# Layer 1's experts, the position-bias table and the combination of rows in a fused four-layer model

## The chip, the cores and the metric

The kernel runs on one core of a Trainium2 chip. The metric is the time in device microseconds (us) of one execution.

## The reference

Four layers work on x of shape (2, 1024, 256), 2048 tokens in 16 tiles of 128. Each layer adds a chain of two blocks to x. Layer 1 is a mixture with shared expert followed by a mixture of eight experts; layer 2 is an attention block with a learned relative bias, followed by a product-key block:

```python
# layer 1, second block: 8 experts, 2 per token, width 512
logits = x @ router_w.T;  topk_logits, topk_idx = top_k(logits, 2);  probs = softmax(topk_logits)
hmid = gelu(einsum('th,efh->etf', x, w1) + b1);  y = einsum('etf,ehf->eth', hmid, w2) + b2
out = einsum('eth,te->th', y, combine)            # combine: probs at the chosen experts
# layer 2, first block: bias of 16 heads from the distance of two positions
pos = arange(-n + 1, n)[:, None]
h = silu(ln(pos @ w0 + b0, g0));  h = silu(ln(h @ w1 + b1, g1));  h = h @ w2 + b2
xn = ln(x, g_norm);  q, k, v = projections of xn;  q = l2norm(q) * q_scale;  k = l2norm(k) * k_scale
sim = q @ k.T * 8 + bias, causal;  out = softmax(sim) @ v;  ln(out @ Wout, g_out)
```

## The kernel before

The kernel is a sequence of phases. Each phase gives every engine its own list of instructions, written by hand; engines wait for each other on semaphores; a barrier over all engines ends a phase. Within a phase the work runs tile by tile through `pipeline(eng, n, unroll, *stages)`: at step t an engine does each of its stages for tile t minus the stage's lag, in the order in which the stages are listed. An engine takes its instructions strictly in that order.

The phases that the change touches, in their order, are these.

**Routing of layer 1's experts** (`route_phase`). GpSimd first gathers the rows that the block before wrote (`Gather.rows`, two indirect transfers per tile, 32 in all), VectorE adds them (`Gather.add`, line 976), TensorE transposes the sum and multiplies it by the router's weights, and VectorE chooses two experts per token for groups of four tiles and computes the slots (`choose`, `slots`; line 1344 writes them). GpSimd then scatters each tile's rows into DRAM at its slots, two indirect transfers per tile (line 1122). SyncE loads all eight experts' weights (8 MB, `Experts.load`) and both biases, each as a row repeated over the 128 partitions.

**Layer 1's expert phase** (`kept_experts_phase`, 39 tiles of 128 slots, each with one expert). SyncE loads the tile's rows and stores its results. TensorE transposes the rows (line 1801), multiplies them as the stationary operand by 512 columns of the expert's first weights (line 1810), transposes the activated result (line 1818), and multiplies it by the second weights (line 1827). VectorE adds the first bias (line 1865), ScalarE does the Gelu (line 1846) and copies both transposes out of PSUM (lines 1841, 1851), VectorE adds the second bias (line 1873). TensorE's order is

```python
            pipeline(pe, n_tiles, 4, (0, transpose_x), (2, transpose_h), (1, hidden), (3, outputs))
```

TensorE and VectorE read the number of the tile's expert into a register for each of these operations from tile 8 on.

**The combination phase** (`combine_phase` with `BiasTable`). GpSimd gathers the experts' output rows again (32 transfers), VectorE adds them to x (32 operations). In the same phase the bias table of layer 2 is made: a perceptron of two layers over 1024 positions in 8 tiles, with VectorE (line 2011, then normalising, lines 1993 to 2004), ScalarE (Silu), TensorE (transposes, line 2050; product, line 2056; last product, line 2062) in turn. The additions of rows stand between the table's steps. SyncE then writes the table to DRAM and spreads it with one transfer, in which each of 16 heads gets 128 rows of 1024 numbers, each row starting one number earlier (line 1972). The attention core reads it from there.

**The null phase of layer 2** (`null_phase`): four small loads on SyncE's queue and some ten short operations. Layer 0 has one too, with three loads.

**The projections of layer 2** (`qkv_phase`): SyncE loads the weights, ScalarE and VectorE fold the gain into them, and then for each tile VectorE normalises the rows, TensorE transposes and multiplies them (line 274, 12 passes), ScalarE and VectorE copy the result out (lines 316, 387), ScalarE squares it, VectorE makes the inverse norms and the keys, GpSimd scales the queries (line 451), and TensorE transposes queries and keys (line 287). The product has one set of three PSUM banks.

The attention core (`core_phase`) comes next. Two other phases are used for comparison. `mlp_experts_phase` is layer 0's expert phase: its weights are the stationary operand, ScalarE adds the bias and activates in one operation per 128 columns (line 1559), and the width is 1024, in two PSUM banks, each with its own signal. `glu_experts_phase` has GpSimd copy each tile's weights (768 columns) out of the resident ones (line 1643).

## Time and profile before

| | |
|---|---|
| time, median of 3 runs (range) | 3152.14 us (3149.24 to 3155.32) |
| time of the profiled execution | 3152.37 us |
| span of its trace | 3150.7 us |
| TensorE matmul busy | 2529.1 us (80%) |
| TensorE weight loads busy | 2025.1 us (64%) |
| VectorE, ScalarE, GpSimd busy | 1592.4, 1336.2, 858.2 us (51%, 42%, 27%) |
| DMA, mean over the span | 95 GB/s |

Engines are named PE (TensorE), PEld (its weight loads), DVE (VectorE), ACT (ScalarE), POOL (GpSimd) and SPq (SyncE's queue) in the profile. Shares over the whole span mix phases that have different limits. Instants in the timeline count from the span's start. In brackets at a row's end stands how long the engine was idle before the row, and what ended the wait. PEclk is the granted clock of TensorE as a share of its full speed. The notation `x16` counts the instructions merged into a row.

### The profile page before, as it was taken

How to read it: one execution, taken by the hardware profiler on the slowest of the kernel's cores; microseconds unless marked ns; L12 is line 12 of the kernel's file. 1: busy time of each engine (PE TensorE's matmuls, PEld its weight loads, DVE VectorE, ACT ScalarE, POOL GpSimd, SP SyncE). 2: the span in 40 equal slices, each digit the busy share in tenths (PEclk: the TensorE clock that was granted, in tenths of full speed). 3: DMA queues.
4: the chain of work that ended last, by engine and by line, in shares of the span. 5: the costliest groups of instructions: out<-in, count | busy, mean ns of one | idle time of the engine just before them, and what ended most of it. 6: DMA issues, size and time to landing. Idle time of an engine off the chain costs nothing. (4 is left out here: it accounts for less than half of the span.)

```text
span 3150.7 us, 56089 instructions
## 1 busy us (share of the span) xinstructions
PE 2529.1 (80%) x16160; PEld 2025.1 (64%) x16161; DVE 1592.4 (51%) x4387; ACT 1336.2 (42%) x3092; POOL 858.2 (27%) x1094
## 2 busy tenths in 40 slices
PE   4799999987877827951669999998689998883695
PEld 2477777766777724641347777776667877782685
DVE  3366666545115251233766666654388886435111
ACT  2366666742221502320336566674344443152221
POOL 0132333312014470031133233331243331345002
PEclk9999999997988958976889999999899999795898
DMA  7022132202663461124002212130200000235585
GB/s 259 30 75 77 61 91 68 83 15 116 248 197 83 140 240 50 56 77 141 6 30 68 81 63 89 62 89 16 77 1 1 0 1 11 94 126 187 196 309 178
DMA packets 146656, 298.72 MB, mean 95 GB/s; under 512 B 20822, under 2 KB 106070, under 8 KB 140224
## 3 DMA queue, kind: packets, MB, share of 16 engines
q1 hardware_dynamic: 134208, 265.00, 24.9%
q0 software_dynamic: 12288, 31.83, 3.3%
q8 instruction: 71, 1.16, 0.2%
q14 instruction: 89, 0.73, 0.1%
HBM read 242.33 MB, written 64.56 MB: 97 GB/s over the span
## 5 line engine op out<-in xcount | busy, mean ns | idle before, releaser
L755 DVE CUSTOM_DVE_ANT_0 prob_l<-ps_l,bias_l,nsn 128x1024 f32<-128x1024 f32 (+3 forms) x256 | 276.8, 1081 | 113.1 <-DVEq L754 66.3
L755 DVE CUSTOM_DVE_ANT_0 cur_sb<-ps_h,bias_s,nsn 128x128 f32<-128x128 f32 (+3 forms) x256 | 139.9, 546 | 241.7 <-DVEq L754 241.2
L830 ACT ACTIVATE prob_l<-prob_l,nmax 128x1024 f32<-128x1024 f32 (+3 forms) x256 | 252.0, 984 | 2.4 <-DVE nmax L755 2.1
L686 PE MATMUL ps_l<-khi,stage 128*128 128x512 f32 (+3 forms) x512 | 240.9, 471 | 0.0
L692 PE MATMUL ps_pt<-ident_sb,prob_l 128*128 128x128 f32 x1664 | 231.8, 276 | 5.3 <-DVE pT_l L763 2.8
L814 ACT ACTIVATE cur_sb<-ps_pt 128x128 f32<-128x128 f32 (+3 forms) x256 | 111.1, 434 | 267.4 <-PE ps_pt L692 267.3
L650 POOL COPY nsn<-nsn 128x4 f32 (+1 forms) x128 | 23.9, 187 | 713.1 <-DVE diff L772 570.6
L659 POOL TENSOR_TENSOR stage<-qo,stage 64x256 fp32r<-64x256 f32 x256 | 201.2, 786 | 46.9 <-POOLq L658 46.9
L692 PEld LDWEIGHTS ps_pt<-ident_sb,prob_l 128*128 128x128 f32 x1664 | 186.7, 141 | 29.4 <-ACT cur_sb L814 13.9
L715 PE MATMUL ps_o<-pT_l,v 128*64 128x256 f32 x1664 | 191.6, 380 | 8.7 <-DVE pT_l L763 8.7
L967 POOL DMA_INDIRECT yg<-slot_outputs,slot x128 | 132.3, 1034 | 239.3 <-PEq L88 200.5
L814 ACT ACTIVATE pT_l<-ps_pt 128x512 f32<-128x512 f32 x256 | 153.1, 598 | 78.6 <-PE ps_pt L692 76.0
L274 PE MATMUL ps_q<-wf,xnT 128*128 128x512 f32 (+1 forms) x384 | 144.0, 527 | 49.8 <-ACT xnT L310 49.8
L1559 ACT ACTIVATE hT<-ps_h,mlp_ws 128x128 f32<-128x128 f32 x312 | 89.1, 369 | 223.3 <-PE ps_h L1532 223.2
L686 PE MATMUL ps_l<-klo,stage 128*128 128x512 f32 (+3 forms) x512 | 181.0, 354 | 0.0
L2176 POOL TENSOR_TENSOR ss<-simx,sim 128x4096 f32<-128x4096 f32 x16 | 113.3, 7084 | 242.2 <-DVE simx L2324 242.2
L680 PE MATMUL ps_l<-km,ident 128*128 128x384 bf16 (+5 forms) x512 | 164.5, 321 | 10.2 <-POOL stage L659 10.2
L715 PEld LDWEIGHTS ps_o<-pT_l,v 128*64 128x64 f32 x1664 | 127.0, 137 | 65.7 <-issue 18.4
L1532 PEld LDWEIGHTS ps_h<-xT,mlp_ws 128*128 128x128 f32 x1248 | 148.8, 196 | 2.8 <-DVE xT L1574 0.9
L274 PEld LDWEIGHTS ps_q<-wf,xnT 128*128 128x128 f32 x384 | 69.6, 199 | 125.1 <-issue 111.6
L1532 PE MATMUL ps_h<-xT,mlp_ws 128*128 128x128 f32 x1248 | 149.3, 279 | 0.1
L830 ACT ACTIVATE cur_sb<-cur_sb,nmax 128x128 f32<-128x128 f32 (+3 forms) x256 | 142.6, 557 | 0.0
(334 smaller groups left out, 6075.4 us busy)
## 6 DMA issues: line engine op xcount, KB each, us to landing
mlp_ws<-in_L_ffn_experts_dram SPq DMA_DIRECT2D x39, 2052.0 KB, 7.5
xs<-slot_rows SPq DMA_DIRECT2D x156, 128.0 KB, 2.1
slot_outputs<-ys SPq DMA_DIRECT2D x156, 128.0 KB, 1.9
slot_rows<-zero_sb SPq DMA_DIRECT2D x1, 16384.0 KB, 51.6
bias_l<-in_fside_16xSxS_dram SPq DMA_DIRECT2D x16, 512.0 KB, 3.5
mlp_w<-in_L_ffn_experts_dram SPq DMA_DIRECT2D x8, 1024.0 KB, 15.0
bias_by_partition<-bias_table SPq DMA_DIRECT2D x1, 8192.0 KB, 36.3
bias_l<-bias_by_partition SPq DMA_DIRECT2D x16, 512.0 KB, 3.3
```

What stands on the lines that cost most here:

```text
L274: ins = pe.matmul(ps_q[:, lo:hi], xnT[:, u % 2, k, :], wf[:, k, lo:hi], start=(k == 0), stop=(k == KD - 1))
L659: gp.tensor_tensor(stage[other, x.b, s, hp], q_t, stage[own, x.b, s, hp].bitcast(F32), ALU.subtract).then_inc(gp_s[s].sem, 1)
L680: pe.matmul(out[:, 0:hi - lo - diagonal], c["ident16"][:], att["km"][:, b, lo:hi - diagonal], start=True, stop=False, skip_group_check=True)
L686: ins = pe.matmul(out, stage[:, b, s, x.h % 2, x.h // 2, :], att[part][:, b * S + lo:b * S + hi], start=False, stop=part == "klo", skip_gr ...
L692: ins = pe.transpose(ps_pt[:, bank, (k - first) * P:(k - first + 1) * P], prob[x.s][:, x.h, k * P:(k + 1) * P], c["ident"][:])
L715: ins = pe.matmul(ps_o[hp * DH:(hp + 1) * DH, s * 2 * P:(s + 1) * 2 * P], att["v"][:, x.b * TB + k, :], pT[s][:, k, hp * 2 * P:(hp + 1) * ...
L755: dve.tensor_tensor_reduce(out=spans(x, prob), in0=scored(x), in1=spans(x, bias), scale=-1.0, scalar=nsn[:, b, s, h:h + 1], op0=ALU.add, o ...
L814: act.activation(pT[x.s][:, 0:n, place(x.h)], ps_pt[:, 0, 0:n * P].rearrange("p (k n) -> p k n", n=P), ACT.Copy).then_inc(act_t[x.s].sem, 1)
L830: act.activation(prob[x.s][:, x.h, 0:x.W], prob[x.s][:, x.h, 0:x.W], ACT.Exp, bias=nmax[:, x.b, x.s, x.h:x.h + 1], scale=-1.0, accum_out=r ...
L967: gp.indirect_dma_start(out=yg[:, k, t, :], out_offset=None, in_=self.ys_dram[0:self.n_slots, :], in_offset=bass.IndirectOffsetOnAxis(ap=s ...
L1532: ins = pe.matmul(o, ws[:, u, k * F + f * P:k * F + (f + 1) * P], xT[:, u % 2, k * P:(k + 1) * P], start=(k == 0), stop=(k == KD - 1))
L2176: gp.tensor_tensor(ss[:, u % 2].rearrange("p h (a b) -> p h a b", b=NK), simx[:].unsqueeze(3).to_broadcast([P, HR, NA, NK]), sim[:, 1].uns ...
```

## The change

Four things are done together.

1. In layer 1's expert phase GpSimd copies the tile's weights and the first bias (one column per 128 hidden units) into a ring of four buffers. The first product takes the weights as the stationary operand and the rows as the moving one, so its result is already transposed; ScalarE adds the bias and does the Gelu in four operations of 128 columns, straight out of PSUM. The transposes of the activated result, the separate bias addition and the second copy go. VectorE copies the transposed rows instead of ScalarE.
2. The bias table is made within the routing phase of layer 1's experts, in steps placed among the routing's own steps on VectorE, ScalarE and TensorE. Router logits share a PSUM tile with the transposes there. Its spread to DRAM is issued by GpSimd as its first instruction of the expert phase.
3. The combination phase between layers 1 and 2 is dropped. Its gathers are issued by GpSimd, and its additions done by VectorE, tile by tile in layer 2's projections, whose lists for these two engines are unrolled. The rows land in two buffers that exist already (`c["cur"]` and `r["acc"]`), and the second serves the attention core as a buffer later.
4. The first bias of all experts is loaded in a layout by partition, in elements of 4 bytes.

```diff
@@ qkv_phase, VectorE and GpSimd
+            def combine(t, u):
+                if gather:
+                    if t == 0:
+                        dve_g.open(dve)
+                    gather.add(dve, t, yg, dve_g)
+
             def moments(t, u):
+                if gather:
+                    dve.wait_ge(dve_g.sem, dve_g.after(f"y{gather.choices - 1}", t))
...
-            stages = [(0, moments), (1, normalised)]
+            stages = [(0, combine), (0, moments), (1, normalised)]
...
-                pipeline(gp, NT, 4, (0, normalised))
+                def fetched(t, u):
+                    gather.rows_of_tile(gp, yg, t)
+
+                if gather:
+                    unrolled(gp, NT, 4, (0, fetched), (4, normalised))
+                else:
+                    pipeline(gp, NT, 4, (0, normalised))
@@ route_phase, TensorE
+            def bias_table(t, u):
+                if table is None:
+                    return
+                if t == 3:
+                    table.turn(pe, 1)
+                if t == 5:
+                    table.second_product(pe)
+                if t == 8:
+                    table.turn(pe, 2)
+                if t == 10:
+                    table.last_product(pe)
+
-            pipeline(pe, NT, NT, (late, turned), (S_AT + 2, down), (L_AT, logits), (S_AT, gate_up), (R_AT, ranks))
+            pipeline(pe, NT, NT, (late, turned), (S_AT + 2, down), (L_AT, logits), (S_AT, gate_up), (R_AT, ranks), (0, bias_table))
@@ route_phase, VectorE
+            def bias_table(t, u):
+                if table is None:
+                    return
+                if t == 1:
+                    table.first_layer(dve)
+                if t == 2:
+                    table.normalise(dve, 1)
+                if t == 4:
+                    table.turned_half(dve, 1)
+                if t == 6:
+                    table.second_layer(dve)
+                if t == 7:
+                    table.normalise(dve, 2)
+                if t == 9:
+                    table.turned_half(dve, 2)
+
             pipeline(dve, NT, NT, (0, combine), (0, norm), (L_AT + 1, logits), (S_AT + 1, hidden), (L_AT + 1, choose),
-                     (R_AT + 1, slots))
+                     (R_AT + 1, slots), (0, bias_table))
@@ kept_experts_phase
+        @block.gpsimd
+        def _(gp):
+            table_dram, spread_dram, spread_done = bias_spread
+            gp.dma_start(spread_dram, bass.AP(table_dram.tensor, table_dram.offset + P - 1,
+                                              [[S + P, H], [-1, P], [1, S]])).then_inc(spread_done, 16)
+            gp_w.open(gp)
+            gp.wait_ge(experts.sem, experts.count)
+
+            def weights(t, u):
+
+                e = experts.of(gp, r, t)
+                gp.wait_ge(pe_y.sem, pe_y.after("y", t - 4))
+                gp.wait_ge(gp_w.sem, gp_w.after("weights", t - 1))
+                gp.sem_inc(gp_w.sem, 1)
+                gp.tensor_copy(b1s[:, u], at(experts.vectors[0], e)).then_inc(gp_w.sem, 1)
+                gp.tensor_copy(ws[:, u], at(experts.w, e)).then_inc(gp_w.sem, 1)
+
+            pipeline(gp, n_tiles, 4, (0, weights))
...
             def hidden(t, u):
-                e = experts.of(pe, r, t)
-                pe.wait_ge(act_x.sem, act_x.after("xT", t))
-
-                pe.wait_ge(dve_h.sem, dve_h.after("pre", t - 2))
-                for k in range(KD):
-                    ins = pe.matmul(ps_h[:, u % 2, 0:F], xT[:, u % 2, k * P:(k + 1) * P],
-                                    at(experts.w, e)[:, k * F:(k + 1) * F], start=(k == 0), stop=(k == KD - 1))
+                pe.wait_ge(dve_x.sem, dve_x.after("xT", t))
+                pe.wait_ge(gp_w.sem, gp_w.after("weights", t))
+                pe.wait_ge(act_h.sem, act_h.after("h", t - 2))
+                for f in range(FC):
+                    for k in range(KD):
+                        ins = pe.matmul(ps_h[:, u % 2, f * P:(f + 1) * P], ws[:, u, k * F + f * P:k * F + (f + 1) * P],
+                                        xT[:, u % 2, k * P:(k + 1) * P], start=(k == 0), stop=(k == KD - 1))
                 ins.then_inc(pe_h.sem, 1)
...
-            pipeline(pe, n_tiles, 4, (0, transpose_x), (2, transpose_h), (1, hidden), (3, outputs))
+            pipeline(pe, n_tiles, 4, (0, transposes), (2, outputs), (1, hidden))
...
             def hidden(t, u):
-                act.wait_ge(dve_h.sem, dve_h.after("pre", t))
-                act.wait_ge(pe_t.sem, pe_t.after("hT", t - 2))
-                act.activation(h[:, u % 2, :], pre[:, u % 2, :], func).then_inc(act_h.sem, 1)
...
+                act.wait_ge(pe_h.sem, pe_h.after("h", t))
+                for f in range(FC):
+                    ins = act.activation(hT[:, u % 2, f * P:(f + 1) * P], ps_h[:, u % 2, f * P:(f + 1) * P], func,
+                                         bias=b1s[:, u, f:f + 1])
+                ins.then_inc(act_h.sem, 1)
```

ScalarE has table steps in the routing too: a root at steps 1 and 6, Silu at 3 and 8, the other half of the turned table at 4 and 9, the last bias at 11. SyncE loads the table's weights ahead of the experts' and stores the table behind them.

## Rows read from the trace of the kernel before

**Rows 1.** Windows view: one stretch of the expert phase, and the combination phase.
```profile
core 0: us, PE busy (x) PEld busy (x) DVE busy (x) ACT busy (x) POOL busy (x), PEclk, DMA share, GB/s
1205.00:1370.00 165.00, 154.27 (x635) 101.83 (x635) 39.09 (x70) 57.22 (x108) 0.00 (x0) 1.00 0.17 54
1386.00:1452.00 66.00, 19.71 (x72) 14.40 (x72) 39.21 (x97) 12.71 (x11) 34.21 (x33) 0.65 0.27 79
```

**Rows 2.** Timeline of layer 1's expert phase: start, length, engine, line, operation.
```profile
1191.76 5.42 SPq L1779 DMA_DIRECT2D xs<-slot_rows  x5
...
1196.46 3.78 PE L1810 MATMUL ps_h<-mlp_w,xT 128*128 128x512 f32 x4
...
1214.64 0.42 DVE L1873 TENSOR_TENSOR ys<-ps_y,mlp_v 128x256 f32<-128x256 f32 x1 [1.04 <-PE ps_y L1827]
...
1369.42 0.42 DVE L1873 TENSOR_TENSOR ys<-ps_y,mlp_v 128x256 f32<-128x256 f32 x1 [1.03 <-PE ps_y L1827]
```

**Rows 3.** Timeline of the combination and null phases.
```profile
1386.26 0.35 SPq L1962 DMA_DIRECT2D w<-in_L_cond_w_dram  x1
...
1452.86 14.90 SPq L474 DMA_DIRECT2D m<-in_mask_BxS_bf_dram  x1
...
1492.82 0.38 SPq L244 DMA_DIRECT2D w<-in_L_cond_Wq_dram  x1
```

**Rows 4.** DMA issues on the page: KB each, us to landing.
```profile
bias_by_partition<-bias_table SPq DMA_DIRECT2D x1, 8192.0 KB, 36.3
```

**Rows 5.** Timeline of the null phase of layer 0.
```profile
10.05 0.35 SPq L474 DMA_DIRECT2D m<-in_mask_BxS_bk_dram  x1
...
18.11 0.38 SPq L244 DMA_DIRECT2D w<-in_L_cond_Wq_dram  x1
```

**Rows 6.** Timeline of the routing of layer 1's experts.
```profile
1131.57 0.18 DVE L1344 CAST slot_out<-rk 128x4 uint32<-128x4 f32 x1
...
1142.97 1.03 POOL L1122 DMA_INDIRECT slot_rows<-cur_sb,slot_out  x1 [0.30 <-issue]
...
1143.44 0.17 DVE L1344 CAST slot_out<-rk 128x4 uint32<-128x4 f32 x1
...
1182.86 0.98 POOL L1122 DMA_INDIRECT slot_rows<-cur_sb,slot_out  x1 [0.30 <-issue]
```

**Rows 7.** Groups by line, VectorE, combination phase: busy us, mean ns.
```profile
L976 DVE SCALAR_TENSOR_TENSOR x_sb<-yg,wt,x_sb 128x256 f32<-128x256 f32 x32 | 14.4, 476 | 0.6
```

**Rows 8.** Timeline of VectorE in the combination phase.
```profile
1406.47 2.29 DVE L2004 TENSOR_TENSOR h<-h,g 128x2048 f32<-128x2048 f32 x1
...
1414.54 1.23 DVE L2016 COPY hT<-ps_bias 128x1024 f32<-128x1024 f32 x1 [3.94 <-PE ps_bias L2050]
...
1424.64 2.29 DVE L2019 TENSOR_TENSOR h<-ps_bias,b 128x2048 f32<-128x2048 f32 x1 [7.05 <-PE ps_bias L2056]
```

**Rows 9.** Groups by line, GpSimd's copies, whole kernel.
```profile
L1643 POOL COPY ws<-glu_w 128x768 f32 x62 | 51.3, 827 | 51.0 <-POOLq L1642 51.0
...
L2169 POOL COPY xs<-cur_sb 128x256 f32 x12 | 15.7, 1311 | 0.0
```

**Rows 10.** Timeline of the MLP expert phase of layer 0.
```profile
842.39 3.62 PE L1543 MATMUL ps_y<-mlp_ws,hT 128*128 128x256 f32 x16
...
845.85 3.73 PE L1532 MATMUL ps_h<-xT,mlp_ws 128*128 128x128 f32 x32
...
849.42 0.38 PE L1522 MATMUL ps_x<-ident_sb,xs 128*128 128x128 f32 x2
...
849.62 1.14 ACT L1559 ACTIVATE hT<-ps_h,mlp_ws 128x128 f32<-128x128 f32 x4 [0.64 <-PE ps_h L1532]
```

**Rows 11.** Timeline of layer 2's projections.
```profile
1597.95 0.91 DVE L387 COPY raw<-ps_q 128x512 f32<-128x512 f32 x2 [0.51 <-PE ps_q L274]
...
1605.29 0.91 DVE L387 COPY raw<-ps_q 128x512 f32<-128x512 f32 x2 [0.41 <-PE ps_q L274]
...
1608.89 5.88 PE L274 MATMUL ps_q<-wf,xnT 128*128 128x512 f32 x12 [1.95 <-ACT xnT L310]
...
1614.32 0.91 DVE L387 COPY raw<-ps_q 128x512 f32<-128x512 f32 x2 [2.19 <-PE ps_q L274]
```

More of the change, by code:

```diff
@@ L216, in qkv_phase @@
         weights, tabled, folded = ph.sem(), ph.sem(), ph.sem()
+        if gather:
+            dve_g = ph.steps(" ".join(f"y{k}" for k in range(gather.choices)))
         dve_0 = ph.steps("stats waited moments")
@@ L532, in core_phase @@
         prob = (ph.sb("prob_l", [P, 4, LONG * P]), spare[0])
-        pT = (ph.sb("pT_l", [P, LONG, 4 * P]), spare[1])
+        pT_l = ph.sb("pT_l", [P, LONG, 4 * P]) if rows is None else rows[:].rearrange("p (k two) d -> p k (two d)", two=2)
+        pT = (pT_l, spare[1])
         oT = ph.sb("oT", [P, 4 * P])
@@ L1095, in _ @@
                     sp.dma_start(dst[:], src_.rearrange("(k p) n -> p k n", p=P)).then_inc(shared_in, 16)
+            if table:
+                table.load(sp)
             if experts is not None:
                 experts.load(sp)
+            if table:
+                table.store(sp)
             if first_weights is not None:
@@ L1717, with __init__ @@
 class Experts:
-    def __init__(self, nc, ctx, name, arrived, w, vectors=()):
+    def __init__(self, nc, ctx, name, arrived, w, columns=None, rows=None):
         E = w.shape[0]
@@ L1762, in kept_experts_phase @@
         stores = [ph.sem() for _ in range(4)]
+        gp_w = ph.steps("expert bias weights")
         pe_x = ph.steps("xT")
-        act_x = ph.steps("xT")
+        dve_x = ph.steps("xT")
         pe_h = ph.steps("h")
-        dve_h = ph.steps("pre")
         act_h = ph.steps("h")
-        pe_t = ph.steps("hT")
-        act_t = ph.steps("hT")
         pe_y = ph.steps("y")
@@ L1874, in outputs, with combine_phase @@
                                   ).then_inc(dve_y.sem, 1)
-            pipeline(dve, n_tiles, 4, (1, hidden), (3, outputs))
-def combine_phase(nc, pool, c, gather, out=None, bias_table=None):
+            pipeline(dve, n_tiles, 4, (0, transposed), (2, outputs))
+def combine_phase(nc, pool, c, gather, out=None):
     G = 4
     with Phase(nc, pool) as ph:
-        yg = ph.sb("yg", [P, gather.choices, NT, D])
+        yg = [ph.sb(f"yg{k}", [P, NT, D]) for k in range(gather.choices)]
         dve_g = ph.steps(" ".join(f"y{k}" for k in range(gather.choices)))
         stored = ph.sem()
-        table = BiasTable(nc, ph, c, *bias_table) if bias_table else None
         block = ph.stack.enter_context(nc.Block())
@@ L2007, in vector, with then, row_moments, first_layer @@
+    def then(self, dve, ins):
+        self.count += 1
+        ins.then_inc(self.v, 1)
+        dve.wait_ge(self.v, self.count)
+    def row_moments(self, dve):
+        for t in range(S // P):
+            ins = dve.bn_stats(self.stats[:, t, :], self.h[:, t, :])
+        self.then(dve, ins)
+        for t in range(S // P):
+            ins = dve.bn_aggr(self.mv[:, t, :], self.stats[:, t, :])
+        ins.then_inc(self.moments, 1)
+    def first_layer(self, dve):
         dve.wait_ge(self.made, 1)
-        then(dve.tensor_copy(self.pos[:], self.pos_i[:]))
+        self.then(dve, dve.tensor_copy(self.pos[:], self.pos_i[:]))
@@ L2020, in vector @@
[L2020 to L2035 removed]
+        for t in range(S // P):
+            ins = dve.scalar_tensor_tensor(self.h[:, t, :], self.rows["w0"][:], self.pos[:, t:t + 1], self.rows["b0"][:],
+                                           ALU.mult, ALU.add)
@@ new lines, in first_layer, with normalise @@
+        self.then(dve, ins)
+        self.row_moments(dve)
+    def normalise(self, dve, n):
+        h = self.h
+        dve.wait_ge(self.rooted, n)
+        self.then(dve, dve.reciprocal(self.rstd[:], self.sd[:]))
+        for t in range(S // P):
+            ins = dve.tensor_scalar(h[:, t, :], h[:, t, :], self.mv[:, t, 0:1], self.rstd[:, t:t + 1], ALU.subtract, ALU.mult)
+        self.then(dve, ins)
+        dve.tensor_tensor(h[:], h[:], self.rows[f"g{n - 1}"][:].unsqueeze(1).to_broadcast([P, S // P, D]),
+                          ALU.mult).then_inc(self.normed, 1)
@@ new lines, in turned_half, with second_layer, root @@
+    def turned_half(self, dve, n):
+        dve.wait_ge(self.turned, n)
+        dve.tensor_copy(self.hT[:, 1, :], self.ps_t[:, 1, :]).then_inc(self.out_t, 1)
+        if n == 2:
+            dve.memset(self.table[:, S:], 0.0).then_inc(self.cleared, 1)
+    def second_layer(self, dve):
+        dve.wait_ge(self.product, 1)
+        self.then(dve, dve.tensor_tensor(self.h[:], self.ps_h, self.rows["b1"][:].unsqueeze(1).to_broadcast([P, S // P, D]), ALU.add))
+        self.row_moments(dve)
+    def root(self, act, n):
+        act.wait_ge(self.moments, n)
+        act.activation(self.sd[:], self.mv[:, :, 1], ACT.Sqrt, bias=self.c["eps"][:, 0:1]).then_inc(self.rooted, 1)
```

299 lines of the change are left out of this document (130 added, 169 removed).

## The prediction

> **What bounds the kernel now.** I read the windows by phase first, then the timeline of each phase that the edit touches, then the groups by line. The kernel is a string of phases with barriers between them, so each has its own bound. In layer 1's expert phase TensorE is busy 154 of 165 us at full clock [rows 1]; finished tiles leave VectorE at 1214.64 and, 33 tiles later, at 1369.42: 4.69 us each [rows 2]. The combination phase is the opposite: TensorE 19.7 of 66 us, no engine above 60% [rows 1]. It is a serial walk through the bias table, from its first load at 1386.26 to the null phase's first load at 1452.86, 66.60 us [rows 3]. The null phase lasts to 1492.82, because its loads stand behind the 8192 KB spread transfer, which takes 36.3 us to land; the load right behind it takes 14.90 us to issue [rows 3, 4]. The same phase in layer 0, with nothing ahead of it, takes 8.06 [rows 5]. The routing phase is bound by GpSimd: 32 gathers, then 32 scatters from 1142.97 to 1182.86, 1.287 us apart, without a pause. So its end is set by when a group's slots are ready against GpSimd's need: group 0's at 1131.75 against 1142.97 (11.2 us to spare), group 1's at 1143.61 against 1142.97 + 10.3 = 1153.3 (9.7) [rows 6].
>
> **Removed.** The combination phase goes: 66.60. The spread moves one phase up, so the null phase's 39.96 becomes layer 0's 8.06 plus 0.5 for a fourth load: 31.4 [rows 3, 5]. Together 98.0.
>
> **The table moved into routing.** VectorE was busy 39.2 us in the combination phase, 14.4 of it the 32 additions [rows 1, 7]: 24.8 us of table work enters its queue in steps 1 to 9, nearly all ahead of group 0's slots (step 8). Behind each of its waits stand the additions, the choice and the slots. I laid the queues out in order. Step 1 can start at 1112; the table's loads go out ahead of the experts' and are there. The first layer takes VectorE to 1119, normalising to 1125.4. At step 4 it waits for Silu and the transposes, 5.8 us in all [rows 8], to 1131.2; at step 6 for the second product, 8.9 us [rows 8] after the halves are copied and TensorE has done its own step 5: 1143.4. The second layer ends at 1149, its normalising at 1155.5, and group 0's slots come at 1158.4, so the scatters start 15.7 us late. Group 1's slots came 11.9 behind group 0's [rows 6]; with the second half to copy and TensorE's last product ahead of the logits they come 15.2 behind, at 1173.6, where GpSimd wants them at 1169.0: 4.7 more. Groups 2 and 3 are in time. Routing: +20.5. Bounds: +14 if group 1 fits too and a little is absorbed, +27 if all of the 26.7 us by which group 0 slips is felt. ScalarE's table switches lie in its idle time. The bias in 4096 pieces of 4 bytes instead of a broadcast is priced by no row; it has 80 us before anything waits for it, so I cost it at nothing; without that cover the start of the expert phase would slip by what is left of it, and I allow 2 us for gathers that it slows.
>
> **The spread on GpSimd's queue.** It is GpSimd's first instruction in the expert phase; the copy of the first tile's weights is queued behind it, and the first product waits for that copy. An indirect transfer of 128 rows costs GpSimd 1.03 us [rows 6], 8.0 ns a row; the spread has 16 x 128 = 2048 rows, 16.4 us. Bounds: the price of one issue, 1 us, and 36, if GpSimd stands until the data has landed [rows 4]. SP's next load took 14.90 us to issue behind these 2048 rows [rows 3], near 16.4, so I take that. GpSimd copies 768 columns in 827 ns [rows 9], hence 2048 in 2.2 at most; with the bias copy and the gaps 2.7. The first product moves from 1196.46 to the phase's start, 1191.4 (its first load is issued at 1191.76) + 16.4 + 2.7 = 1210.5 [rows 2]: +14.0. At 1 us the copy is there before the row tiles: 0. At 36: +33.6.
>
> The Trainium skill (DMA: Bandwidth & Descriptors, section Anatomy of one DMA, SWDGE (gpsimd) path) says that generating descriptors is small and that many can be emitted before the cost shows. By that page the spread costs GpSimd next to nothing and the sum is 14.0 lower; no row here shows a plain transfer issued by GpSimd.
>
> **The expert tile.** TensorE loses the four transposes and the dynamic expert reads; the first product becomes 16 passes of 128 columns. The MLP phase has this form: 32 such passes run from 845.85 to 849.42, so 16 take 1.79; 16 passes of the second product run from 842.39 to 845.85, so 8 take 1.73 [rows 10]; two transposes 0.22. TensorE's work falls to 3.74. But its order is transposes(t), outputs(t-2), hidden(t-1): a tile's outputs follow its own hidden product with one pair of transposes between. ScalarE's four Gelu wait for the whole product (one signal), start 0.20 behind it and take 1.14 [rows 10]; TensorE's next pass runs later by an allowance of 0.16. In the MLP phase a second bank covers this; here nothing does. Period: 1.79 + 0.20 + 1.14 + 0.16 + 1.73 = 5.02 for 4.69, +0.33 on 38 periods, 12.5, less about 2.8 for a drain that is one step shorter: +9.7. GpSimd's 2.7 per tile and VectorE's two operations hide below 5.02; with ScalarE's part covered the tile would take 3.74.
>
> **Projections of layer 2.** VectorE gets two additions per tile, 0.48 each [rows 7] and their waits: 1.04. The loop runs TensorE, VectorE's copy, ScalarE, TensorE: 7.34 us from copy to copy (1597.95 to 1605.29), or 9.03 (to 1614.32) where the clock falls and twelve passes take 5.88, four steps of the twelve in the timeline; in the fast step VectorE waits only 0.41 for its copy [rows 11]. 7.34 - 0.41 + 1.04 is 7.97, some 7.9 with waits that close: VectorE becomes the bound in the eight fast ones. 8 x 0.55 = 4.4, two additions before the first transposes 2.1, the ends 1.5: +8. Bounds: +2, the start alone, and +18, if every step goes the slow way. Gathers take GpSimd 2.6 a tile, in its wait for VectorE, and the first is due before the weights are folded.
>
> **Sum.** -98.0 + 20.5 + 14.0 + 9.7 + 8 = -45.8. The profiled execution took 3152.37 us (span 3150.7), the median is 3152.14: one frame. Forecast 3106.5.
>
> **Rivals.**
> - The spread's issue is cheap on GpSimd: 3092.5. No row prices it; against it stand 8 ns a row. 0.27.
> - GpSimd stands until the spread has landed, +33.6 for +14.0: 3126. SP's queue did stand behind it. 0.10.
> - The clock falls in the expert phase. TensorE idles 1.28 of 5.02 us there; in the projections it idles 1.95 and one step in three costs 1.69 more [rows 11]. 13 such tiles, +22: 3128.5. Against: shorter gaps. 0.13.
> - ScalarE's part is covered and a tile takes 3.74: 38 x 1.28 less, 3058. Against: the one signal. 0.04.
> - The other side: the weight copies bind. That outweighs the gain from 45.8 / 39 + 5.0 = 6.2 us a tile. One row points there: 256 columns in 1.31 us [rows 9], 10.5 for 2048, 11.0 a tile, 39 x 6.0 = +234: 3340. But those copies follow a long addition beside a busy VectorE, and the 768-column ones, in an expert phase like this, took 827 ns on the mean of all. 0.04.
>
> The Trainium skill (SBUF — State Buffer, section Who interferes with whom) holds that VectorE shuts GpSimd out only with two SBUF inputs or in a two-port mode. VectorE's operations in this phase read PSUM, so by that page the last rival falls; no run has shown it.
>
> **Numbers.** Forecast 0.40, rivals as given, 0.02 left. All terms at their low ends give -98 + 14 + 0 + 9.7 + 2 = -72 (3080), all at their high ends +13. Eight in ten lie in 3080 to 3132. A measurement of this kernel tells 0.2%, 6.3 us, from no change: faster 0.94, same 0.02, slower 0.04.
>
> **What would show it.** No combination phase and a null phase of 9 us; first scatter near 1158 and a pause before the ninth; the first hidden product some 19 us behind the expert phase's first load; a period of 5.0 with TensorE waiting 1.3 a tile for ScalarE; fast projection steps at 7.9. I am wrong if routing grows by under 10 us, if the period is far from 5.0, or if GpSimd's first weight copy is immediate or 30 us late.

## The result, and the profile after

The changed kernel takes 3100.57 us (median of 4 runs, 3096.48 to 3102.75), the kernel before 3150.69 beside it (4 runs). The ratio is 0.9841 with a 95% interval of 0.9819 to 0.9863: 50.1 us less, 1.6%. The profiled execution took 3096.48 us, span 3094.8, so the two profiled spans are 55.9 apart. Timelines put 51.4 of that in the stretch that the edits touch (the attention core's first bias load moved from 1642.88 to 1591.44); the other 4.5 lie behind it, in phases that the edits leave alone, and are not counted as theirs.

Timeline of the routing and the start of the expert phase, changed kernel (start, length, engine, line, operation, idle time before it and what ended it):

```profile
1143.58 1.00 POOL L1002 DMA_INDIRECT yg<-slot_outputs,slot  x1 [0.30 <-issue]
...
1158.50 0.17 DVE L1417 CAST slot_out<-rk 128x4 uint32<-128x4 f32 x1
...
1159.63 1.10 POOL L1165 DMA_INDIRECT slot_rows<-cur_sb,slot_out  x1 [15.06 <-DVEq L1418]
...
1174.14 0.17 DVE L1417 CAST slot_out<-rk 128x4 uint32<-128x4 f32 x1
...
1175.16 1.17 POOL L1165 DMA_INDIRECT slot_rows<-cur_sb,slot_out  x1 [4.93 <-DVEq L1418]
...
1205.52 0.98 POOL L1165 DMA_INDIRECT slot_rows<-cur_sb,slot_out  x1 [0.31 <-issue]
...
1214.52 3.93 SPq L1875 DMA_DIRECT2D xs<-slot_rows  x5
1214.82 1.10 POOL L1890 DMA_DIRECT2D bias_by_partition<-bias_table  x1 [8.32 <-POOLq L91]
...
1216.04 1.91 POOL L1902 COPY ws<-mlp_w 128x2048 f32<-128x2048 f32 x1
...
1218.05 3.34 PE L1924 MATMUL ps_h<-xT,ws 128*128 128x128 f32 x16 [0.37 <-DVE xT L1962]
...
1302.56 1.99 PE L1933 MATMUL ps_y<-ws,hT 128*128 128x256 f32 x8 [1.02 <-ACT hT L1947]
1304.39 1.95 PE L1924 MATMUL ps_h<-xT,ws 128*128 128x128 f32 x16
...
1306.37 1.14 ACT L1947 ACTIVATE hT<-ps_h,b1s 128x128 f32<-128x128 f32 x4 [3.87 <-PE ps_h L1924]
...
1307.57 1.99 PE L1933 MATMUL ps_y<-ws,hT 128*128 128x256 f32 x8 [1.01 <-ACT hT L1947]
...
1423.61 0.35 SPq L505 DMA_DIRECT2D m<-in_mask_BxS_bf_dram  x1
...
1432.87 0.38 SPq L257 DMA_DIRECT2D w<-in_L_cond_Wq_dram  x1
```

The reader is to see four things against [rows 2, 3, 6]. GpSimd stands 15.06 us between its last gather and its first scatter, which before followed each other at once, and 4.93 ahead of group 1. The 8192 KB spread costs GpSimd 1.10 us, and the first product starts 3.53 us behind the first row load (4.70 before). A tile takes 1302.56 to 1307.57, 5.01, and TensorE waits 1.0 of it for ScalarE. The combination phase is gone, and the null phase takes 9.26 us.

Windows of the changed kernel: most of the expert phase, and two steps of layer 2's projections.

```profile
core 0: us, PE busy (x) PEld busy (x) DVE busy (x) ACT busy (x) POOL busy (x), PEclk, DMA share, GB/s
1230.00:1400.00 170.00, 133.75 (x868) 118.95 (x869) 28.13 (x67) 38.40 (x135) 66.59 (x66) 1.00 0.24 79
1471.14:1478.75 7.61, 4.81 (x20) 2.67 (x19) 7.22 (x18) 3.38 (x7) 3.94 (x3) 1.00 0.12 36
1478.75:1487.91 9.16, 7.02 (x25) 3.77 (x24) 7.32 (x19) 4.25 (x10) 3.94 (x3) 0.81 0.10 29
```

TensorE is busy for 79% of the expert phase, where it was 93% [rows 1], and the clock stays at 1.00, the 2.4 GHz level. In a fast step of the projections VectorE is now busy 7.22 of 7.61 us; the rest is gaps of up to 0.15 between its own operations.

A table from the timelines, with those of the experiments below. Routing is the first gather to the last scatter, the expert phase its first row load to the next phase's first load, the projections their first load to the core's first bias load. Only the first row has a combination phase, of 66.60 us. A time with (1) is that of one execution.

| kernel | time, us | ratio to before | routing | expert phase | null | projections |
|---|---|---|---|---|---|---|
| before | 3150.69 | 1 | 82.52 | 194.50 | 39.96 | 150.06 |
| changed | 3100.57 | 0.9841 (0.9819 to 0.9863) | 104.73 | 209.09 | 9.26 | 158.57 |
| outputs_last | 3053.14 | 0.969 (0.9673 to 0.9706) | 105.97 | 164.92 | 9.25 | 159.04 |
| old_tile | 3096.72 (1) | | 104.65 | 202.38 | 9.16 | 158.86 |
| spread_on_sync | 3127.04 (1) | | 105.80 | 238.90 | 9.24 | 159.21 |
| table_spaced | 3087.46 | 0.9795 (0.9779 to 0.9811) | 96.45 | 209.97 | 9.58 | 158.31 |
| copied_twice | 3071.08 (1) | | 104.92 | 175.08 | 8.94 | 161.66 |
| spread_by_pairs | 3066.22 | 0.9717 (0.9697 to 0.9738) | 104.50 | 177.72 | 8.97 | 161.87 |
| best | 3051.44 | 0.9673 (0.9656 to 0.9691) | 87.70 | 177.03 | 8.98 | 161.55 |
| adds_on_gpsimd | 3097.38 (1) | | 104.42 | 208.99 | 9.31 | 160.93 |
| eight_row_tiles | 3048.51 | 0.9668 (0.9642 to 0.9693) | 105.41 | 154.58 | 9.25 | 161.63 |
| best_2 | 3025.51 | 0.9604 (0.9588 to 0.9619) | 88.26 | 154.21 | 9.28 | 158.60 |
| all_heads_pieces | 3044.63 (1) | | 107.01 | 154.58 | 9.08 | 161.67 |
| best_3 | 3029.20 | 0.9602 (0.9581 to 0.9623) | 88.43 | 154.70 | 9.10 | 159.47 |

Single times move by several us: executions of the kernel before, taken beside these runs, took 3142.70 to 3163.98. The phase columns are steadier, and most verdicts below rest on them. The projections are an example of why: where their lists are the changed kernel's, they take 158.3 to 161.9, with five to seven of their steps over 8.5 us, where the clock is lower for a part.

### The profile page after: what moved, and what is told of

Read it like the earlier page. It is cut to its first block and busy times, and to the rows that moved or that the text cites. A ratio compares the mean times of both kernels' runs of the same rounds, so it can differ in the third digit from the quotient of the medians.

```text
span 3094.8 us, 56173 instructions
## 1 busy us (share of the span) xinstructions
PE 2512.4 (81%) x16472; PEld 2048.1 (66%) x16472; DVE 1589.5 (51%) x4387; ACT 1318.4 (43%) x3132; POOL 940.5 (30%) x1173
## 5 line engine op out<-in xcount | busy, mean ns | idle before, releaser
L712 PE MATMUL ps_l<-km,ident 128*128 128x384 bf16 (+5 forms) x512 | 164.4, 321 | 10.2 <-POOL stage L691 10.2
L1002 POOL DMA_INDIRECT yg<-slot_outputs,slot x96 | 100.2, 1044 | 228.6 <-PEq L88 200.0
L1632 PE MATMUL ps_y<-mlp_ws,hT 128*128 128x256 f32 x624 | 144.9, 386 | 0.0
L1632 PEld LDWEIGHTS ps_y<-mlp_ws,hT 128*128 128x128 f32 x624 | 117.9, 194 | 15.4 <-issue 0.2
L724 PE MATMUL ps_pt<-ident_sb,cur_sb 128*128 128x128 f32 x640 | 116.8, 280 | 6.2 <-ACT pT_l L846 3.0
## 6 DMA issues: line engine op xcount, KB each, us to landing
slot_rows<-zero_sb SPq DMA_DIRECT2D x1, 16384.0 KB, 51.4
bias_by_partition<-bias_table POOLq DMA_DIRECT2D x1, 8192.0 KB, 36.6
```

The costliest lines, as they stand in the source:

```text
L712: pe.matmul(out[:, 0:hi - lo - diagonal], c["ident16"][:], att["km"][:, b, lo:hi - diagonal], start=True, stop=False, skip_group_check=True)
L724: ins = pe.transpose(ps_pt[:, bank, (k - first) * P:(k - first + 1) * P], prob[x.s][:, x.h, k * P:(k + 1) * P], c["ident"][:])
L1002: gp.indirect_dma_start(out=yg[k][:, t, :], out_offset=None, in_=self.ys_dram[0:self.n_slots, :], in_offset=bass.IndirectOffsetOnAxis(ap=s ...
L1632: ins = pe.matmul(ps_y[:, u % 2, 0:D], hT[:, u % 2, f * P:(f + 1) * P], ws[:, u, w2 + f * D:w2 + (f + 1) * D], start=(f == 0), stop=(f == ...
```

## The experiments

**Outputs last.** TensorE's order within a step, in the expert phase only:

```
-            pipeline(pe, n_tiles, 4, (0, transposes), (2, outputs), (1, hidden))
+            pipeline(pe, n_tiles, 4, (0, transposes), (1, hidden), (2, outputs))
```

> Only the order of TensorE's steps in layer 1's expert phase changes: transposes(t), hidden(t-1), outputs(t-2), so that a tile's Gelu has another tile's outputs, transposes and first product beside it. Theory (the 5.04 us period is a ring through ScalarE, 1.2 us of it TensorE's wait): the period falls to TensorE's own work in the changed kernel's timeline, 1.83 from outputs to first product, 1.78 to the transposes and 0.2, so 3.8 us; 38 periods save about 46 us, 3100.6 to 3054. Rival A (the ring only moves: GpSimd's copy of 2.1 us plus its wait for a buffer, or SyncE's row loads, bind next): the period stops between 4.2 and 4.8, 3065 to 3090. Rival B (the 5.04 was not ScalarE's part): the period stays within 0.1 of 5.04 and the time within 0.2% of 3100.6.

Measured: the phase 164.92 for 209.09 us, the kernel 3053.14. The theory's number to the microsecond. Windows and timeline of this kernel:

```profile
1245.00:1370.00 125.00, 125.00 (x867) 116.40 (x866) 25.56 (x66) 38.17 (x134) 64.58 (x64) 0.99 0.22 72
```

```profile
1228.65 0.36 SPq L1875 DMA_DIRECT2D xs<-slot_rows  x1
...
1241.81 0.69 PE L1915 MATMUL ps_x<-ident_sb,xs 128*128 128x128 f32 x2 [7.63 <-DMA xs<-slot_rows]
...
1249.82 1.89 PE L1933 MATMUL ps_y<-ws,hT 128*128 128x256 f32 x8
...
1253.55 1.89 PE L1933 MATMUL ps_y<-ws,hT 128*128 128x256 f32 x8
```

TensorE is busy in all of 125 us, and a tile takes 3.73. So the order alone took 1.3 us off each tile, and the wait for ScalarE's four Gelu is gone; neither the weight copies nor the row loads hold the steady tile (rival A). The timeline also shows what came next: once the tiles are fast, one row load, issued at 1228.65, is not there when TensorE wants it, and finished tiles are 13.7 us apart at that place instead of 3.7. That is 10.0 us, which the expectation did not have. Its number came out right because the period fell further than it said (from 5.04 to 3.73, not 3.8) and the drain is shorter (the last two gaps are 3.52 and 1.72 us, where the changed kernel keeps 5.07).

**The old tile form.** The expert phase of the kernel before in the changed kernel, with the spread on GpSimd:

```
-                kept = Experts(..., columns=a["L1_ffn_b1"], rows=a["L1_ffn_b2"])
+                kept = Experts(..., (a["L1_ffn_b1"], a["L1_ffn_b2"]))
 @@ kept_experts_phase: as before, and
+        @block.gpsimd
+        def _(gp):
+            gp.dma_start(spread_dram, bass.AP(...)).then_inc(spread_done, 16)
```

> Layer 1's expert phase is the one of the kernel before (rows stationary, four transposes of the result, no copies of weights, first bias loaded by broadcast), with the spread still issued by GpSimd as the phase's first instruction; all else as changed. Theory (the new tile form costs the phase 14.6 us as traced, 209.1 against 194.5 from first load to next phase's first load): the phase takes 194.5 again, the period is 4.69, and the kernel comes to about 3086. Rival (what grew is the phase's surroundings, the spread's transfer beside the row loads among them): the phase stays above 200 us. If the bias load in 4-byte elements matters at all, the routing phase shortens here by more than 1 us.

Measured: the phase takes 202.38, between the two kernels: 7.9 us over the phase before and 6.7 under the changed one. The rival was right, and it says where 7.9 us come from:

```profile
1235.46 0.36 SPq L1868 DMA_DIRECT2D xs<-slot_rows  x1
...
1238.49 0.42 DVE L1968 TENSOR_TENSOR ys<-ps_y,mlp_v 128x256 f32<-128x256 f32 x1 [1.03 <-PE ps_y L1922]
...
1245.77 0.69 PE L1896 MATMUL ps_x<-ident_sb,xs 128*128 128x128 f32 x2 [7.52 <-DMA xs<-slot_rows]
...
1252.82 0.42 DVE L1968 TENSOR_TENSOR ys<-ps_y,mlp_v 128x256 f32<-128x256 f32 x1 [1.07 <-PE ps_y L1922]
```

A row load issued while the spread is under way takes over 10 us (12.5 in the changed kernel, below; the 27 us that the expectations further on give it are wrong), and finished tiles are 14.33 us apart instead of 4.7. That is 9.6 us, of which a faster start gives 1.8 back: the first finished tile comes 16.1 us behind the first row load for 17.95. So the spread is not free with this tile form; in the changed kernel, whose tiles take 5.0 for another reason, it costs only 1.2 (one gap of 6.25), and the other 13.4 of its 14.6 us belong to the tile form. The routing takes 104.65 here and 104.73 in the changed kernel: loading the bias in 4-byte elements costs nothing that the profile shows.

**The spread on SyncE.** The same transfer, moved ahead of the row loads in the other list:

```
 @block.gpsimd
-            gp.dma_start(spread_dram, bass.AP(...)).then_inc(spread_done, 16)
 @block.sync
+            sp.dma_start(spread_dram, bass.AP(...)).then_inc(spread_done, 16)
```

> The spread is issued by SyncE ahead of the row loads, not by GpSimd; nothing else changes. Theory (the 14.90 us that a load took to issue behind the 2048-row transfer belongs to SyncE's hardware queue, and GpSimd's software queue has no such stand): the row loads come 15 us late, the first product moves from 3.5 to about 19 us behind the phase's first instruction, and the kernel takes about 3115. Rival (the stand came from the barrier or from loads that read the same rows, not from the queue): the row loads go out at once and the time stays within 0.2% of 3100.6.

```profile
1210.85 0.69 SPq L1882 DMA_DIRECT2D bias_by_partition<-bias_table  x1
...
1211.85 35.09 SPq L1875 DMA_DIRECT2D xs<-slot_rows  x5
...
1245.02 1.12 PE L1915 MATMUL ps_x<-ident_sb,xs 128*128 128x128 f32 x4 [58.82 <-DMA xs<-slot_rows]
```

DMA view of the spread and of the first row load behind it, us to landing:

```profile
bias_by_partition<-bias_table SPq DMA_DIRECT2D x1, 8192.0 KB, 33.8
xs<-slot_rows SPq DMA_DIRECT2D x1, 128.0 KB, 33.1
```

The first product comes at 1246.3, 35 us behind the phase's first instruction, and the kernel takes 3127. The theory had the place right and the size wrong. On the same queue the first row load does not only stand for its issue (12.66 us here, 14.90 in [rows 3]); it is issued 1.0 us behind the spread, lands 33.1 us later, and so comes 0.3 us after the spread's end. Issued by GpSimd, the spread leaves the first five row loads alone.

**The table's steps spaced.** Steps of the bias table within the routing, with the same work:

```
 VectorE:  first layer 1, normalise 2 -> 3, half 4 -> 7, second layer 6 -> 14,
           normalise 7 -> 17, half 9 -> (ScalarE copies both halves)
 TensorE:  turn 3 -> 5, second product 5 -> 11, turn 8 -> 19, last product 10 -> 20
 ScalarE:  root 1 -> 2, Silu 3 -> 4, half 4 -> 6, root 6 -> 15, Silu 8 -> 18, halves 9 -> 19, last bias 11 -> 20
```

> The bias table's steps within the routing are set further apart and behind the slots of groups 0 and 1: VectorE first layer at step 1, normalising at 3, turned half at 7, second layer at 14, second normalising at 17 (the second pair of halves is copied by ScalarE alone); TensorE's second product at step 11, its last two at 19 and 20. The same work is done. Theory (routing grew by 22 us because group 0's slots stand behind waits and work that need not be ahead of them; 9 us of GpSimd's slack was unused): group 0's slots come near 1140, the first scatter at once behind the last gather (no wait of 15 us), and one pause of about 6 us is left ahead of group 2; the last scatter comes about 8 us later than in the kernel before, in place of 22.7, and the kernel takes about 3086. Rival (VectorE's 24.8 us of work bind wherever it stands): the last scatter comes over 18 us late and the time is within 0.2% of 3100.6. Rival (the chain's length binds: the table ends after the last scatter): the scatters end early but the expert phase starts no more than 6 us earlier than in the changed kernel.

```profile
1147.77 1.00 POOL L1002 DMA_INDIRECT yg<-slot_outputs,slot  x1 [0.30 <-issue]
1149.07 1.02 POOL L1165 DMA_INDIRECT slot_rows<-cur_sb,slot_out  x1 [0.30 <-issue]
...
1153.63 9.49 PE L2140 MATMUL ps_bias<-w,hT 128*128 128x256 f32 x32
...
1179.27 0.98 POOL L1165 DMA_INDIRECT slot_rows<-cur_sb,slot_out  x1 [9.82 <-DVEq L1428]
```

The first scatter follows the last gather at once, as the theory has it, but the pause ahead of group 2 is 9.82 and not 6: group 2's logits stand behind 9.49 us of second product in TensorE's list, and VectorE waits. Routing 96.45, 8.3 under the changed kernel and not 14. The time, 3087.46 for 3086 expected, fits better than its reason: the median is 13.1 under the changed kernel, of which the routing shows 8.3 (the profiled execution took 3093.70). Neither rival holds: the work fits, its order cost.

**Weights copied twice**, on top of outputs last:

```
+                gp.tensor_copy(again[:], at(experts.w, e)).then_inc(gp_w.sem, 1)
                 gp.tensor_copy(ws[:, u], at(experts.w, e)).then_inc(gp_w.sem, 1)
```

> Outputs last, with GpSimd copying each tile's weights once more, into a buffer that nobody reads. Theory (the copy costs 1.89 us and hides until GpSimd's tile is longer than TensorE's 3.74): GpSimd needs 0.15 + 0.13 + 2 x 1.9 = 4.1 us a tile, the period becomes 4.1 to 4.2, and the phase grows by 33 x 0.4 = 14 us over outputs last, to about 3068. Rival (copies disturb VectorE's or TensorE's access to the buffers): the period is well over 4.3. Rival (GpSimd's price per copy grows when it never rests): copies over 2.1 us.

The phase grows by 10.2 us to 175.08 (14 expected, and 3068 for the 3071.08 of this one execution): 1.8 ahead of the first product, which now waits for two copies, and 8.1 in the tiles. From the sixteenth on, when the ring's lead is used up, tiles take 3.93 to 4.25. Windows:

```profile
1300.00:1370.00 70.00, 68.41 (x445) 59.74 (x443) 13.32 (x35) 19.39 (x68) 65.86 (x52) 1.00 0.20 64
```

GpSimd is busy 65.86 of 70 us, and each copy still takes 1.89. The theory holds and neither rival does. The copies bind only when GpSimd's tile passes TensorE's: here it is 4.09 on the mean for two copies, 0.31 beside them. By these numbers, as an estimate, a single copy would have to take 3.4 us, and not 1.89, before it costs anything at 3.73 a tile.

**The spread in pieces of two heads**, on top of outputs last: eight DMAs ahead of the copies of tiles 4, 6, ... 18.

```
+                if 0 <= h < H and h % 2 == 0:
+                    gp.dma_start(spread_dram[h:h + 2], bass.AP(table_dram.tensor, table_dram.offset + h * (S + P) + P - 1,
+                                                               [[S + P, 2], [-1, P], [1, S]])).then_inc(spread_done, 16)
```

> On top of the reordered TensorE steps (outputs last), GpSimd issues the spread not whole at the start of the expert phase but two heads at a time (1 MB, an eighth of it) ahead of the weight copies of tiles 4, 6, ... 18; GpSimd's list is unrolled for it. Theory (the transfer costs nothing at its issue but holds the next row loads for 27 us behind it: one gap of 13.7 us between finished tiles in place of 3.7, so 10 us): each piece holds the queues about 4.6 us (36.6 / 8), less than the two tiles (7.5 us) between pieces and less than the lead of the row loads, so no gap is over 5 us and the kernel comes to 3053 - 10 = 3043. Rival (row loads are late whenever pieces are under way): eight gaps of 1 to 2 us, and 3049 to 3053.

A miss: 177.72 for the phase, 12.8 us worse than the whole spread. The pieces delay tiles by 0.5 to 2 us each, and the last costs 13.6 us alone. DMA view of the phase (1214 to 1393 us), of the last piece, and of the software queue from 1228 to 1231 us, when only the first piece was under way on it:

```profile
q0 software_dynamic: 16512, 8.45, 16.2%
...
bias_by_partition<-bias_table POOLq DMA_DIRECT2D x8, 1024.0 KB, 12.7
...
bias_by_partition<-bias_table POOLq DMA_DIRECT2D x1, 1024.0 KB, 26.0
...
q0 software_dynamic: 34, 0.14, 12.4%
```

One line of its timeline:

```profile
1302.85 1.05 POOL L1896 DMA_DIRECT2D bias_by_partition<-bias_table  x1 [18.79 <-issue]
```

GpSimd stood 18.79 us before an issue that takes 1.05. And one piece kept 12.4% of the 16 DMA engines' time, two sixteenths. Against the whole spread the size, the place and the shape had all changed; the shape was the next suspect.

The 12.7 us to landing is too kind to this form. All eight pieces count on one semaphore, and at 1235.5, where the profile puts the landing of the first, only 108 packets of 4 KB had gone through the queue, where a piece has 256. The last piece has none behind it: its 26.0 us are the price of one.

**First combination of the gains**: outputs last, pieces of two heads, the table spaced, and the second product in quarters at steps 8, 9, 12 and 13.

> Three edits together: outputs last, the spread in eight pieces, and the table's steps spaced in the routing as before, with TensorE's second product split into quarters at steps 8, 9, 12 and 13 (the wait of VectorE for it was 6 us in the spaced version). Theory: the spaced routing took 8.3 us off the changed kernel's; the split takes the pause ahead of group 2's scatters from 9.5 us to 3 at most, 6 more; with 3043 for the other two the kernel comes to 3043 - 8 - 6 = 3029. Rival (the chain of the table ends too late for the split to help): 3035. Rival (the gains do not add): over 3040.

3051.44, where 3029 was expected: the rival that the gains do not add was nearest, and the phases say why. The routing went to 87.70, so the quarters took 8.8 us more off it; the expert phase took 177.03, 12 us more than with the whole spread, where the pieces were to save 10.

**The additions on GpSimd**, in layer 2's projections of the changed kernel:

```
-            stages = [(0, combine), (0, moments), (1, normalised)]
+            stages = [(0, moments), (1, normalised)]
-                    unrolled(gp, NT, 4, (0, fetched), (4, normalised))
+                    unrolled(gp, NT, 4, (0, fetched), (2, combine), (6, normalised))
```

Each addition becomes a product and an addition there.

> The changed kernel with the combination's two additions per tile in layer 2's projections done by GpSimd (a product with the weight, then an addition, each twice) instead of VectorE; GpSimd gathers, adds two tiles behind, and normalises six behind. Theory (VectorE, busy without a gap for 7.62 us, is the bound of the fast steps): the fast step falls to the 7.34 us of the kernel before or a little under, and the projections shorten by 8 x 0.28 plus the 2.1 us at the start, 154 us in place of 158.6. Rival (GpSimd becomes the bound: 2.6 for two gathers, 1.9 for normalising, four operations of 256 columns at 0.3 to 1.3 each): steps of 8 us or more and projections over 160 us. Rival (the loop is not VectorE's): no change within 1 us.

Steps of 7.43 to 7.47 instead of 7.62, so VectorE was the bound. But a tile then has 1.9 + 2.4 + 3.3 us of work for GpSimd, which takes 7.90 us from tile to tile without a rest; the first copy of results comes 3.8 us later (28.6 us behind the first load for 24.8), and the projections take 160.9. Nothing is gained: the rival that GpSimd becomes the bound is the nearest.

**Eight row tiles**, on top of outputs last: the spread whole, ahead of the fourth weight copy, and twice the ring.

```
-        xs = ph.sb("xs", [P, 4, D])
+        xs = ph.sb("xs", [P, 8, D])
-            pipeline(sp, n_tiles, 4, (0, load), (4, store))
+            pipeline(sp, n_tiles, 8, (0, load), (8, store))
```

> Outputs last, the spread whole again but issued by GpSimd ahead of its fourth weight copy (some 7 us into the phase), and a ring of eight row tiles in place of four: SyncE loads eight tiles ahead, and its stores are issued eight tiles behind in its list. Theory (the only cost of the spread is that row loads issued behind it land 27 us later, and the row ring of four covers 11 to 15 us of that): nine row tiles are in or under way ahead of it, 9 x 3.74 = 34 us of work, so the gap of 13.7 us between finished tiles is gone and the kernel comes to 3053 - 10 = 3043. Rival (stores, held behind the spread too, bind instead because the output ring has four buffers): a gap of 5 to 15 us at VectorE's addition, waiting for a store, and 3048 to 3060.

```profile
1254.13 0.42 DVE L1970 TENSOR_TENSOR ys<-ps_y,mlp_rows 128x256 f32<-128x256 f32 x1 [4.14 <-DMA slot_outputs<-ys]
```

The phase takes 154.58, 10.3 less: the theory. Of the rival's wait for a store a little is seen, as in this line, in two gaps of 4.65 and 5.20, made good behind it. The time, 3048.51, has the widest range of all (3039.88 to 3057.05), and its interval (0.9642 to 0.9693) overlaps that of outputs last (0.9673 to 0.9706), so the time alone does not show the gain. The phase does. In the profiled execution, 3053.24 for 3052.98 with outputs last, what was gained there was lost again where this edit touches nothing: the routing ended 2.7 later, the projections took 2.6 more, and the rest lies behind them.

**The second combination**: this, with the table spaced and the product in quarters.

> The same with the table's steps spaced and the second product in quarters, whose routing took 87.7 us from the first gather to the last scatter in the version before this one, against 104.7 in the changed kernel. Theory: 3043 - 17 = 3026. Rival (stores bind as above): 3031 to 3043.

3025.51, 0.9604 of the kernel before, for 3026 expected.

**Pieces of all heads**: as the pieces of two heads, but 16 partitions of all 16 heads each.

```
-                    gp.dma_start(spread_dram[h:h + 2], ... [[S + P, 2], [-1, P], [1, S]])
+                    q = h // 2 * (P // 8)
+                    gp.dma_start(spread_dram[:, q:q + P // 8, :], ... [[S + P, H], [-1, P // 8], [1, S]])
```

> The spread in eight pieces at the same places as before, but each piece is 16 partitions of all 16 heads (outermost dimension 16) and not all partitions of two heads (outermost dimension 2). Theory (the pieces of two heads were slow because of their shape: 12.7 us to landing for 1 MB, 17.5 thousand packets in the phase's software queue where the whole spread leaves 3.0, and the last one stood 18.8 us on GpSimd for it): a piece lands in 4.6 us (36.6 / 8) or a little more, none stands, no gap between tiles is over 5 us, the phase takes some 155 us in place of 177.7, and the kernel takes 3043. Rival (pieces of 1 MB are slow whatever their shape, since GpSimd makes their descriptors): 12 us to landing and 3060 or more again.

DMA view of the phase (1213 to 1369 us), and of the software queue from 1224.5 to 1227 us, with one piece under way:

```profile
q0 software_dynamic: 2176, 8.39, 15.5%
...
bias_by_partition<-bias_table POOLq DMA_DIRECT2D x8, 1024.0 KB, 5.9
...
q0 software_dynamic: 237, 0.97, 95.3%
```

The same 1 MB, the same places in GpSimd's list, 5.9 us to landing for 26.0, and the phase 154.58 for 177.72. Shape alone, then. The last line says how: one piece now has 95.3% of the 16 engines' time, where one of two heads had 12.4%. The 14336 packets more in the other form are no smaller rows. They bring 0.06 MB, 4 bytes each; the rows go in packets of 4 KB in both.

**The third combination**: the same in place of the ring of eight.

> The version with the spaced table, outputs last, a ring of four row tiles, and the spread in pieces of 16 partitions. Theory: 3026, the same as with the ring of eight row tiles and the whole spread, since both leave TensorE nothing to wait for. Rival as above: 3045 or more.

3029.20, 0.9602, with an interval that holds the second combination's. Its windows show that the expert phase has nothing left but TensorE's own work:

```profile
1225.00:1320.00 95.00, 95.00 (x659) 88.42 (x659) 19.55 (x50) 29.64 (x104) 53.18 (x56) 1.00 0.40 133
```

## Why the prediction was right, and where it was not

The direction and the time were right (3106.5 forecast, 3100.57 measured, range 3080 to 3132), but the sum holds one wrong term and one that is too small, which cancel in part. That the time came within 6 us is in part luck: one term was 15.2 us too large, and the others together 9.1 too small.

- **Removed**: 98.0 forecast, 97.3 measured. 66.60 went whole; the null phase takes 9.26 where I had 8.56.
- **Routing**: +20.5 forecast, +22.2 measured. Group 0's slots were done at 1158.67 (forecast 1158.4) and group 1's at 1174.31 (1173.6); the pause ahead of group 1 is 4.93 (4.7). Some 1.4 us come from scatters that took longer than the 1.287 apart. The mechanism, waits and work queued ahead of the slots, is shown by the spaced table: the same work in another order, with the second product in quarters, took 16.3 to 17.0 us off.
- **The spread on GpSimd's queue**: the step that failed. I took 8.0 ns a row from indirect transfers [rows 6], 16.4 us, and +14.0 for the first product. It took 1.10 us, and the first product came 1.2 us earlier than before, relative to the phase's first load. The rival that the issue is cheap was right on this term, and by the prediction's own sign it was wrong here: the first weight copy starts at 1216.04, right behind the issue. The price of 8.0 ns a row came from an indirect transfer, and a plain one of 2048 rows does not pay it. The Trainium skill (DMA: Bandwidth & Descriptors, section Anatomy of one DMA, SWDGE (gpsimd) path) says that many descriptors can be emitted before their cost shows, which agrees with the 1.10.
- **What the spread costs instead** was in no part of the prediction. The transfer of 8192 KB takes 36.6 us to land and most of the DMA engines' time meanwhile, and a row load among it lands late. In the changed kernel this costs 1.2 us and is covered by the slow tile. DMA view of the changed kernel from 1226 to 1232 us:

```profile
q0 software_dynamic: 457, 1.87, 98.5%
q1 hardware_dynamic: 3, 0.00, 0.1%
issues: line engine op xcount, KB each, median us to landing
slot_outputs<-ys SPq DMA_DIRECT2D x1, 128.0 KB, 10.6
xs<-slot_rows SPq DMA_DIRECT2D x1, 128.0 KB, 12.5
```

The store was issued at 1228.19 and the row load at 1229.47, so this stretch does not show how the two queues share; from 1232 to 1236 us both move packets:

```profile
q0 software_dynamic: 280, 1.15, 86.6%
q1 hardware_dynamic: 201, 0.19, 14.0%
```

- **The expert tile**: +9.7 forecast, +15.8 measured. The period was right, 5.04 for 5.02, and so was its cause. What was mis-sized is the drain, -2.8: the start did become 3.7 us shorter (9.52 from the first product to the first finished tile, 13.25 before), but the kernel before ended fast, its last tiles 4.3 to 1.7 us apart, 5.2 us under the steady pace, and the new order keeps 5.07 to the end. That makes +1.4. The period gives 38 x 0.35 = 13.3, the spread's gap 1.2.
- **Projections**: +8 forecast, +8.5 measured: fast steps at 7.62 (forecast 7.9, 7.34 before), and the first copy of results 3.9 us later, where I had 2.1 and 1.5 for the ends. The other 4.6 are in the steps: the fast ones cost half of what was forecast, and five run slow for four before.

The measured terms: -97.3 + 22.2 + 0.1 + 14.6 + 8.5 = -51.9 (the 14.6 are -1.2 for the first product, 15.8 for the tiles), and the routing began 0.45 later: -51.4, as traced. The clock did not fall in the expert phase (1.00 there, TensorE idle for 1.0 us of 5.0). The weight copies took 1.89 each and bound nothing; the Trainium skill (SBUF — State Buffer, section Who interferes with whom) lets them run free beside VectorE's reads of PSUM, and all 39 copies of the changed kernel lie between 1.890 and 1.907 us.

The gain of 50 us left 75 more in place (3100.57 to 3025.51). The phases show 44 of them in the order of TensorE's steps, 16 in the order of the table's and 10 in the spread; the other 5 lie outside the phases of the table.

## What to carry to other kernels

When a product's result goes through another engine before the next product reads it, put the next tile's product between the two in TensorE's list; look at the wait in one steady tile, since an average of 79% busy does not say that one line's order costs a quarter. A big transfer moved to a cheap place is still paid by the small ones beside it: count how many microseconds of loads are in hand when it starts, and cut it into pieces whose outermost dimension has sixteen entries. Work moved into another phase's lists costs by what is queued behind it, so place each step behind the last thing that has a deadline before it, and cut a long one into parts.

## What the hardware showed that I had not expected

- A plain DMA of 2048 rows of 4 KB costs GpSimd 1.10 us to issue, as much as an indirect one of 128 rows (1.00). But with eight pieces of the bad shape the last issue stood 18.79 us, until 1302.85, when the seventh (issued at 1275.13, 27.3 us to landing) had landed; what it waited for in the queue was not tried.
- The shape of a transfer of the same size set its speed: 1 MB with outermost dimension 2 landed in 26.0 us (the last piece), with 16 in 5.9. The Trainium skill (DMA: Bandwidth & Descriptors, section Why a DMA increments its semaphore by 16 and not by 1) says that the outermost dimensions decide how many DMA engines a transfer runs on, which agrees with what the traces show: with one piece under way its queue had 12.4% of the 16 engines' time in the one form and 95.3% in the other. In the packet records two packets of 4 KB are in flight at a time in the first and mostly sixteen in the second, each for 159 ns (median) in both.
- Queues of different engines share the DMA engines, as the Trainium skill (DMA: Bandwidth & Descriptors, section Issuing engines are not separate DMA queues) states: beside the spread a row load of 128 KB took 12.5 us for a median of 2.0, and while both moved, its queue got 201 packets through beside 280 of the spread, which are four times as long. On the same queue as the spread the first row load took 33.1 us.
